# Row maxima in pairs of heads, exponentials head by head, and one accumulator for two sets of four heads

## The chip, the cores and the metric

The kernel runs on one core of one Trainium2 chip. The metric is the device time of one launch in microseconds, the median of a few runs. TensorE (PE) multiplies into PSUM, which has eight banks of 512 float32 a partition; VectorE (DVE) and ScalarE (ACT) read it; GpSimd (POOL) works on SBUF and issues the indirect transfers; SyncE (SP) issues the others.

## The reference, cut to what matters

Two layers, each with attention and a mixture of experts, over 32 sequences of 256 tokens of width 128, with 16 heads of width 8. Layer 0 adds a position bias to the scores, has an output projection and two experts a token; layer 1 has one expert a token.

```
for layer in (0, 1):
    mod = silu(c) @ wmod                       # sa, ca, ga, sb, cb, gb per sequence
    h = layernorm(x) * (1 + ca) + sa           # layer 1: a second layernorm inside attention
    q, k, v = projections of h                 # 16 heads of 8
    scores = q @ k.T * scale (+ bias)          # 256 x 256 a head
    x = x + ga * (softmax(scores) @ v ...)     # layer 0: then @ W_out
    h = layernorm(x) * (1 + cb) + sb
    x = x + gb * experts(h)                    # top 2 of 8, or top 1 of 8
```

## The kernel before, in words

Attention of a layer runs in ticks, one for each sequence, and each tick works on several sequences at once: the functions that take an offset get the sequence at(0), at(-1), at(1) and so on. Every engine has its own hand-written order of steps for a tick (the functions tick), and semaphores alone tie the engines together. All steps of an engine run in that order; a step that waits holds up all behind it.

The softmax of a head is computed in two passes. In the first (scores_a, at(0)) TensorE makes the scores with queries on the partitions, one head into one PSUM bank of two (A); VectorE takes the row maxima of each head (row_max, L869). After each eight heads VectorE splits the negated maxima into two bf16 parts (split_max), TensorE turns them (turn_max), ScalarE copies them out (max_rows), and SP sends them as two more rows of the matmul operand (stack_max, L529). In the second pass (scores_b, at(-1)) TensorE makes the transposed scores, from which the maxima are already subtracted through these rows, two heads into a two-bank buffer of two (Bp); ScalarE takes the exponentials of both at once (exps, L722) into probs. Layer 0 adds a product for the bias near the diagonal (L1147).

Then, for each four heads, weigh (L1159) multiplies by the values, whose 32 columns a head are 8 values, a one and zeros, so that four heads fill the 128 partitions of one half of M1; ScalarE copies that out (head_sums, L729); TensorE turns it (turn_heads, L1167) into the other half; and VectorE divides by the sums (normalise, L891 and L895). There is one M1, so the weigh of a set waits for the normalise of the set before.

Other steps of the tick that the text speaks of: first_stats, added_stats, inner_stats, second_stats and rms_moments (moments of rows, through aggregate); first_norm, outer_norm, inner_norm, second_norm (L824) and rms_norm; split_qk on GpSimd, which splits q and k of at(1) into bf16 parts for stack_up (L523); modulate and scatter on GpSimd; residual (L918); choose_first, choose_second, weigh_choices and place, which choose experts and count rows on VectorE. place ends its reading of M0 with the update of run (L1008), after which turn_max(at(0), 0) may write M0. TensorE's order around the start of a tick:

```
a_pass(0, 1)
chunk(0)                    # scores_b of heads 0 and 1 of at(-1); waits for stack_max's rows
a_pass(2)
heads_step(weigh, -2, 3)
...
a_pass(3)
chunk(1)
if at(1):
    ...
    project_qk(*at(1))
a_pass(4)
```

VectorE chains dependent steps with a semaphore (Chain.link, settle). In layer 1, where the next maximum's number is in MIDST, settle first issues that maximum and waits behind it, so that the gap is filled.

The expert stages use the same PSUM buffers for other products and are not changed but for the buffers' names.

## Time and profile before

| what | us |
|---|---|
| median of 3 runs | 2255.24 |
| lowest and highest of them | 2250.59, 2255.43 |
| the profiled execution's own time | 2244.62 |
| its span | 2242.8 |
| busy in the span: PE, DVE, ACT, POOL | 1757.3, 1661.7, 1038.4, 879.3 |
| attention of layer 0, about | 60 to 830 |
| attention of layer 1, about | 1155 to 1980 |

In the rows below an instruction's line is given as L and its number. Windows and timelines count from the span's start. Matmuls are pipelined: the time shown for one includes its way through the array, and consecutive ones overlap.

### The profile page before, as it was taken

What the parts mean: (1) busy time and instruction counts of PE and PEld (TensorE: products, weight loads), DVE (VectorE), ACT (ScalarE), POOL (GpSimd) and SP (SyncE); (2) the same over time, 40 slices, a digit from 0 to 9 for tenths busy, and PEclk for the clock granted to TensorE, in tenths of its full rate; (3) what the DMA queues carried; (4) which work ended last, traced back from release to release, by engine and by line L of the source; (5) the groups of instructions that cost most, each with busy time, mean ns of one, the idle gap of its engine ahead of it and who ended that gap; (6) DMA issues with size and microseconds to landing.
All of it is one profiled execution on the core that took longest, in us unless ns stands there. A gap on an engine that the chain in (4) does not pass through costs nothing. (4 is left out here: it accounts for less than half of the span.)

```text
span 2242.8 us, 55810 instructions
## 1 busy us (share of the span) xinstructions
PE 1757.3 (78%) x14626; PEld 1227.0 (55%) x14626; DVE 1661.7 (74%) x5861; ACT 1038.4 (46%) x1967; POOL 879.3 (39%) x932
## 2 busy tenths in 40 slices
PE   2588888888888847999935777878878788719997
PEld 1355555655555626999832444444444444407775
DVE  3478888888888845666626888898888888724453
ACT  0266666666666631222212555555655656603322
POOL 0224444444443333444423444444444444203333
PEclk7699999999999978999976999898998988959999
DMA  4344434343434313222245545555455454243332
GB/s 139 50 64 71 72 69 73 70 69 70 72 71 68 67 48 74 70 68 68 64 132 84 96 98 106 101 100 108 98 102 109 95 103 103 57 145 93 95 94 62
DMA packets 267157, 190.47 MB, mean 85 GB/s; under 512 B 26081, under 2 KB 257283, under 8 KB 266327
## 3 DMA queue, kind: packets, MB, share of 16 engines
q1 hardware_dynamic: 251738, 154.75, 35.4%
q0 software_dynamic: 15360, 35.03, 5.2%
q8 instruction: 26, 0.43, 0.1%
q14 instruction: 33, 0.26, 0.1%
HBM read 94.68 MB, written 53.18 MB: 66 GB/s over the span
## 5 line engine op out<-in xcount | busy, mean ns | idle before, releaser
L869 DVE TENSOR_REDUCE mx<-A 128x2 f32<-128x512 f32 x1024 | 691.6, 682 | 125.9 <-PE A L1124 94.7
L722 ACT ACTIVATE probs<-B 128x1024 f32<-128x1024 f32 x512 | 524.0, 1023 | 378.9 <-PE B L1144 205.5
L1124 PE MATMUL A<-stack 126*128 126x256 bf16 x2048 | 406.2, 286 | 162.6 <-DVE mx L869 126.5
L1144 PE MATMUL B<-stack 128*128 128x256 bf16 x2048 | 370.9, 285 | 27.2 <-DMA stack<-mrow 27.1
L1124 PEld LDWEIGHTS A<-stack 126*128 126x128 bf16 x2048 | 160.8, 99 | 340.1 <-DVE mx L869 262.5
L1159 PE MATMUL M<-probs,vals 128*32 128x256 f32 x4096 | 294.7, 405 | 23.3 <-DVE On L895 15.1
L1144 PEld LDWEIGHTS B<-stack 128*128 128x128 bf16 x2048 | 201.2, 103 | 86.1 <-issue 22.4
L631 POOL DMA_INDIRECT gathered<-h,slot_in x192 | 187.2, 975 | 154.6 <-DVE slot_in L1016 108.9
L618 POOL TENSOR_TENSOR h<-xn,back_rows 128x256 f32<-128x256 f32 x64 | 46.3, 723 | 503.5 <-DVE xn L824 503.5
L1563 PE MATMUL A<-w2s,hid 128*128 128x128 f32 x1792 | 230.4, 278 | 8.9 <-issue 8.9
L1563 PEld LDWEIGHTS A<-w2s,hid 128*128 128x128 f32 x1792 | 211.8, 192 | 18.2 <-issue 13.2
L1554 PE MATMUL B<-xtT,w1s 128*128 128x256 f32 x896 | 216.6, 395 | 5.2 <-DVE xtT L1440 2.1
L1369 POOL DMA_INDIRECT expert_out<-yt,row_dest x144 | 138.0, 959 | 177.0 <-DVE yt L1475 142.7
L1159 PEld LDWEIGHTS M<-probs,vals 128*32 128x32 f32 x4096 | 128.1, 113 | 116.3 <-issue 56.8
L1554 PEld LDWEIGHTS B<-xtT,w1s 128*128 128x128 f32 x896 | 168.2, 194 | 40.2 <-issue 16.3
L1147 PE MATMUL B<-dist,slope_ident 128*128 128x128 bf16 x1024 | 183.3, 219 | 0.0
L1523 ACT ACTIVATE hid<-B 128x1024 f32<-128x1024 f32 x72 | 73.7, 1024 | 227.9 <-PE B L1554 227.9
L594 POOL TENSOR_TENSOR parts<-qk,ones_col 128x512 bf16<-128x512 f32 x64 | 66.4, 1037 | 257.7 <-ACT qk L700 115.9
L1366 POOL DMA_INDIRECT out<-yt,row_dest x80 | 84.5, 1057 | 170.8 <-DVE yt L1480 147.2
L729 ACT ACTIVATE heads<-M 128x256 f32<-128x256 f32 x256 | 97.9, 383 | 107.2 <-PE M L1159 104.8
L1527 ACT ACTIVATE hid<-B,b 128x256 f32<-128x256 f32 x160 | 62.7, 474 | 174.3 <-PE B L1554 138.2
L668 ACT ACTIVATE rs<-mv,eps_col 128x2 f32<-128x2 f32 x192 | 56.1, 292 | 138.4 <-DVE mv L810 92.2
(190 smaller groups left out, 2847.5 us busy)
## 6 DMA issues: line engine op xcount, KB each, us to landing
stack<-parts SPq DMA_DIRECT2D x768, 64.0 KB
xt<-gathered SPq DMA_DIRECT2D x112, 132.0 KB, 2.2
probs<-gathered SPq DMA_DIRECT2D x40, 256.0 KB, 2.7
w<-in_w SPq DMA_DIRECT2D x4, 2048.0 KB
back_rows<-mod_rows SPq DMA_DIRECT2D x64, 128.0 KB, 3.3
x_mid<-X SPq DMA_DIRECT2D x64, 128.0 KB, 2.0
Y<-expert_out SPq DMA_DIRECT2D x64, 128.0 KB
X<-in_x SPq DMA_DIRECT2D x32, 128.0 KB, 2.9
```

What stands on the lines that cost most here:

```text
L631: pool.indirect_dma_start(gathered[l], bass.IndirectOffsetOnAxis(ap=slot_in[u][:, c, t:t + 1], axis=0), (h3 if l else h2)[u][:, t, :], Non ...
L722: act.activation(probs[c % 4][:, :, :, :], Bp[c % 2][:, :, :, :], ACT.Exp, scale=EXP_SCALE[l][c // 4]).then_inc(b_exp.handle, 1)
L729: act.activation(heads[g % 2][:, :], M1[:, 0:S], ACT.Copy).then_inc(o_read.handle, 1)
L869: dve.tensor_reduce(mx[u][:, h, :], A[h % 2][:, :, :], AX.X, ALU.max).then_inc(a_max.handle, 1)
L1124: ins = pe.matmul(A[h % 2][:, t, :], stack[u][0:n, h, 0, t * P:(t + 1) * P], stack[u][0:n, h, 1, :], start=True, stop=True)
L1144: ins = pe.matmul(Bp[c % 2][:, j, t, :], stack[u][:, h, 1, t * P:(t + 1) * P], stack[u][:, h, 0, :], start=True, stop=(l == 1))
L1147: ins = pe.matmul(Bp[c % 2][:, j, t, t * P:(t + 1) * P], slope_ident[:, h % HH, :], dist[:, :], start=False, stop=True)
L1159: ins = pe.matmul(M1[VW * j:VW * j + VW, 0:S], vals[u][:, t, 4 * g + j, :], probs[(2 * g + j // 2) % 4][:, j % 2, t, :], start=(t == 0), s ...
L1366: ins = pool.indirect_dma_start(expert_out[l], dest, yt[u][:, t, :], None, bounds_check=B * S - 1, oob_is_err=False)
L1369: ins = pool.indirect_dma_start(expert_out[l], dest, yt[u][:, t, :], None)
L1554: ins = pe.matmul(dst[:, f, :], w1s[u][:, f * P:(f + 1) * P], xtT[u][:, :], start=True, stop=True)
L1563: ins = pe.matmul(A[u][:, t, 0:D], hid[u][:, f, t * P:(t + 1) * P], w2s[u][:, f, :], start=(f == 0), stop=(l == 0 and f == FC - 1))
```

## The change

The buffers change places: A (scores for the maxima) becomes two buffers of two banks, Bp (scores for the exponentials) two of one bank. scores_a and row_max take two heads at once, so a tick has eight reductions of 1024 columns and not sixteen of 512. scores_b and exps take one head, so a tick has sixteen exponentials of 512 columns and not eight of 1024. Two weigh steps of four heads now add into one accumulator: the second set reads its values through a window that lies 16 columns earlier, so that its 8 values and its one land in partitions 16 to 24 of each group of 32. So head_sums, turn_heads and normalise run twice a tick for eight heads each, not four times for four, and only every second weigh waits for a normalise. The order of heads in the weights is permuted to fit. All three tick orders are rewritten, and MIDST and the counts of chained steps with them. A cut of the diff:

```diff
-DVE_MARKS = (36, 41)
-MIDST = (2, 4, 5, 7, 8, 10, 11, 13, 14)
+DVE_MARKS = (34, 39)
+MIDST = (1, 2, 4, 5, 7)
...
-        A = [ctx.enter_context(nc.psum_tensor(f"A{n}", [P, NT, S], F32)) for n in range(2)]
-        Bp = [ctx.enter_context(nc.psum_tensor(f"B{n}", [P, 2, NT, S], F32)) for n in range(2)]
+        wide = [ctx.enter_context(nc.psum_tensor(f"A{n}", [P, 2, NT, S], F32)) for n in range(2)]
+        single = [ctx.enter_context(nc.psum_tensor(f"B{n}", [P, NT, S], F32)) for n in range(2)]
...
+            def exps(b, k, u, h):
+                act.wait_ge(b_scores.handle, b_scores.after(b, h + 1))
+                c, g4 = h // 2, h // 4
+                if h % 2 == 0:
+                    act.wait_ge(pv.handle, pv.after(b, g4 - 1) if g4 >= 2 else pv.after(b - 1, g4 + 3))
+                act.activation(probs[c % 4][:, h % 2, :, :], Bp[h % 2][:, :, :], ACT.Exp,
+                               scale=EXP_SCALE[l][h // HH]).then_inc(b_exp.handle, 1)
...
-                chunk(0)
-                step(head_sums, -2, 3)
+                exp(0)
+                step(head_sums, -2, 1)
                 step(second_h, -3)
+                exp(1)
                 layer(0, first_rsqrt, 2)
-                chunk(1)
+                exp(2)
...
-                dve.tensor_reduce(mx[u][:, h, :], A[h % 2][:, :, :], AX.X, ALU.max).then_inc(a_max.handle, 1)
+                dve.tensor_reduce(mx[u][:, 2 * c:2 * c + 2, :].rearrange("p j t -> p (j t)"),
+                                  A[c % 2][:, :, :, :].rearrange("p j t s -> p (j t) s"), AX.X, ALU.max)\
+                    .then_inc(a_max.handle, 1)
...
                 step(split_max, -1, 1)
                 maxima(0, 1)
-                step(normalise, -2, 2)
+                layer(0, first_stats, 2)
                 maxima(1, 1)
-                layer(0, first_stats, 2)
-                maxima(2, 2)
                 layer(0, first_norm, 2)
                 layer(1, added_stats, 2)
-                maxima(4, 1)
-                step(normalise, -2, 3)
-                maxima(5, 1)
+                maxima(2, 1)
+                step(normalise, -2, 1)
                 step(read_logits, -3)
                 layer(1, residual, -2)
-                maxima(6, 1)
+                maxima(3, 1)
+                step(split_max, 0, 0)
                 layer(0, choose_first, -3)
                 layer(1, second_stats, -2)
                 layer(1, outer_norm, 2)
-                maxima(7, 1)
-                step(split_max, 0, 0)
-                maxima(8, 1)
-                step(normalise, -1, 0)
+                maxima(4, 1)
                 layer(1, modulate_rows, 2)
                 layer(1, gated_base, 0)
-                maxima(9, 1)
                 layer(0, choose_second, -3)
                 layer(1, choose_first, -3)
-                maxima(10, 1)
+                maxima(5, 1)
                 layer(0, residual, -2)
                 layer(1, inner_stats, 2)
-                maxima(11, 1)
                 layer(0, second_stats, -2)
                 layer(1, second_norm, -2)
-                maxima(12, 1)
-                step(normalise, -1, 1)
+                maxima(6, 1)
+                step(normalise, -1, 0)
                 step(weigh_choices, -3)
-                maxima(13, 1)
                 layer(1, rms_moments, -2)
                 step(place, -3)
-                maxima(14, 1)
+                maxima(7, 1)
                 layer(0, second_norm, -2)
                 layer(1, inner_norm, 2)
-                maxima(15, 1)
                 layer(1, rms_norm, -2)
...
                 for t in range(NT):
                     for j in range(4):
-                        ins = pe.matmul(M1[VW * j:VW * j + VW, 0:S], vals[u][:, t, 4 * g + j, :],
+                        first = (HH * q + 4 * s + j) * VW
+                        ins = pe.matmul(M1[VW * j:VW * j + VW, 0:S], vals[u][:, t, first:first + VW],
                                         probs[(2 * g + j // 2) % 4][:, j % 2, t, :],
-                                        start=(t == 0), stop=(t == NT - 1), tile_position=(0, VW * j))
+                                        start=(q == 0 and t == 0), stop=(q == 1 and t == NT - 1), tile_position=(0, VW * j))
...
-                a_pass(0, 1)
-                chunk(0)
-                a_pass(2)
+                a_pass(0)
+                b_pass(0)
+                b_pass(1)
+                a_pass(1)
                 heads_step(weigh, -2, 3)
...
-                a_pass(3)
-                chunk(1)
+                b_pass(2)
                 if at(1):
                     m0_read((h2T_read, -3))
                     project_qk(*at(1))
-                a_pass(4)
-                heads_step(turn_heads, -2, 3)
-                a_pass(5)
+                b_pass(3)
+                a_pass(2)
+                heads_step(turn_heads, -2, 1)
                 if at(-3):
                     m0_read((qk_f32, 1))
                     gate(*at(-3))
-                chunk(2)
-                a_pass(6)
+                b_pass(4)
+                b_pass(5)
+                a_pass(3)
                 if at(-1):
                     m0_read((logits_read, -3), (qk_f32, 1))
                     turn_max(*at(-1), 1)
                 heads_step(weigh, -1, 0)
-                a_pass(7)
-                chunk(3)
+                b_pass(6)
                 if at(0):
                     m0_read((mT_read, -1, 2), (qk_f32, 1))
                     project_v(*at(0))
-                a_pass(8)
-                heads_step(turn_heads, -1, 0)
+                b_pass(7)
+                a_pass(4)
```

## Rows read from the trace of the kernel before

**Rows 1.** Windows of both attention stages: window, length, busy time (count) by engine, PEclk, DMA, GB/s

```profile
205.00:700.00 495.00, 429.88 (x4354) 290.88 (x4358) 438.28 (x1442) 306.47 (x570) 214.83 (x220) 1.00 0.42 71
1280.00:1876.00 596.00, 480.74 (x4020) 284.17 (x4023) 531.76 (x1845) 348.63 (x700) 268.77 (x300) 0.90 0.51 103
```

**Rows 2.** Groups by line: layer 0's maxima, all small reductions, layer 1's exponentials and head_sums

```profile
L869 DVE TENSOR_REDUCE mx<-A 128x2 f32<-128x512 f32 x351 | 239.4, 687 | 27.0 <-PE A L1124 21.4 <-DVE xn L824 0.3
...
L956 DVE TENSOR_REDUCE r<-lg 128x2 f32<-128x16 f32 x64 | 10.4, 162 | 0.0
...
L722 ACT ACTIVATE probs<-B 128x1024 f32<-128x1024 f32 x200 | 204.8, 1024 | 168.7 <-PE B L1144 167.8
L729 ACT ACTIVATE heads<-M 128x256 f32<-128x256 f32 x100 | 38.3, 383 | 38.7 <-PE M L1159 38.4
```

**Rows 3.** Timelines of layer 1, VectorE, SP's queue and TensorE: start, duration, instruction, idle before

```profile
1518.51 0.16 DVE L1008 TENSOR_TENSOR run<-run,M 128x8 f32<-128x8 f32 x1
...
1521.23 0.69 DVE L869 TENSOR_REDUCE mx<-A 128x2 f32<-128x512 f32 x1
...
1524.39 0.69 DVE L869 TENSOR_REDUCE mx<-A 128x2 f32<-128x512 f32 x1 [0.90 <-PE A L1124]
...
1526.09 0.69 DVE L869 TENSOR_REDUCE mx<-A 128x2 f32<-128x512 f32 x1 [0.61 <-PE A L1124]
...
1529.17 0.68 DVE L869 TENSOR_REDUCE mx<-A 128x2 f32<-128x512 f32 x1
...
1542.32 0.16 DVE L1008 TENSOR_TENSOR run<-run,M 128x8 f32<-128x8 f32 x1
...
1519.81 0.69 SPq L529 DMA_DIRECT2D stack<-mrow  x1
...
1521.94 0.61 PE L1144 MATMUL B<-stack 128*128 128x256 bf16 x4 [0.52 <-DMA stack<-mrow]
...
1525.66 0.38 PE L1124 MATMUL A<-stack 126*128 126x256 bf16 x2
...
1530.95 0.38 PE L1124 MATMUL A<-stack 126*128 126x256 bf16 x2
```

**Rows 4.** Timeline of VectorE in one tick of layer 0

```profile
500.23 0.69 DVE L869 TENSOR_REDUCE mx<-A 128x2 f32<-128x512 f32 x1
...
501.81 0.47 DVE L819 BATCH_NORM_STATS2 st<-X 128x6 f32<-128x128 f32 x2
502.44 0.25 DVE L810 BATCH_NORM_AGGREGATE mv<-st 128x2 f32<-128x6 f32 x2 [0.16 <-DVEq L111]
502.75 1.29 DVE L869 TENSOR_REDUCE mx<-A 128x2 f32<-128x512 f32 x2
...
504.85 0.69 DVE L869 TENSOR_REDUCE mx<-A 128x2 f32<-128x512 f32 x1 [0.30 <-PE A L1124]
505.46 0.20 DVE L891 RECIPROCAL rsum<-M 128x8 f32<-128x8 f32 x1
...
505.83 0.68 DVE L869 TENSOR_REDUCE mx<-A 128x2 f32<-128x512 f32 x1
...
507.24 0.69 DVE L869 TENSOR_REDUCE mx<-A 128x2 f32<-128x512 f32 x1 [0.65 <-PE A L1124]
...
520.92 0.59 DVE L824 TENSOR_SCALAR xn<-X,mv,rs 128x128 f32<-128x128 f32 x2
```

**Rows 5.** Timelines of layer 0 over two ticks: VectorE, SP's queue, TensorE

```profile
204.34 0.59 DVE L824 TENSOR_SCALAR xn<-X,mv,rs 128x128 f32<-128x128 f32 x2
...
218.88 3.99 SPq L523 DMA_DIRECT2D stack<-parts  x6
...
227.53 0.39 PE L1124 MATMUL A<-stack 126*128 126x256 bf16 x2 [0.36 <-DMA stack<-parts]
```

**Rows 6.** Windows within one tick of layer 1, columns as in rows 1

```profile
1508.00:1514.00 6.00, 3.46 (x37) 1.78 (x34) 5.57 (x22) 2.58 (x5) 0.25 (x1) 0.99 0.61 98
1514.00:1520.50 6.50, 5.93 (x35) 2.80 (x36) 6.13 (x27) 2.81 (x8) 1.93 (x3) 0.50 0.67 144
```

203 lines of the change are left out of this document (103 added, 100 removed).

## The prediction, made before the change was run

> **What bounds the kernel now.** I read the windows first, the two attention stages by themselves, then the groups by line, then the timelines of one tick of either layer. In the windows the reader is to see VectorE busy for nine tenths of both stages (438 of 495 us, 532 of 596), TensorE for less, and TensorE's granted clock at 1.00 in layer 0 but 0.90 in layer 1 [rows 1]. The lines give the tick: 351 maxima at 16 a tick make layer 0's 495 us some 21.94 ticks of 22.56 us, and 200 exponentials at 8 a tick make layer 1's 596 us 25 ticks of 23.84 us [rows 1, 2]. The expert stages change only in the names of their buffers.
>
> Nine tenths busy is not yet a bound. In layer 1 the timeline closes a loop [rows 3]. VectorE's place ends its update of run at 1518.67; the row of maxima goes out on SP's queue at 1519.81; TensorE stands 0.52 us at the first exponential scores until that transfer is in, at 1521.94. Behind it, in TensorE's order, come the scores of heads 2 and 3, a weigh, a turn, more exponential scores and a projection; head 4's scores start at 1525.66, and VectorE takes their maximum at 1526.09, having waited 0.90 us for head 3 and 0.61 for head 4. From 1518.67 that is 7.42 us. Then VectorE works nearly without a pause up to the next place, which ends at 1542.48: 16.39 us. The sum, 23.81, is the tick. So layer 1 is set by 7.42 us in which TensorE and a transfer lead, and 16.39 in which VectorE does.
>
> Layer 0 has another loop, over two ticks. Its last VectorE step but one, second_norm, releases GpSimd, which modulates, scatters, waits for the scatter and only then splits the next q and k; SP issues the stack transfers, and head 0's scores of the tick after next wait for them. From second_norm's end (204.93) to those scores (227.53, idle 0.36 on that DMA) it is 22.6 us [rows 5]. About 0.55 later the first maximum starts, and from a first maximum (500.23) to second_norm's end (521.51) are 21.28 us [rows 4]. (22.6 + 0.55 + 21.28) / 2 = 22.2, against 22.56 measured: this loop nearly sets the tick.
>
> **The change part by part, for one tick.**
>
> *Maxima.* Two reductions in a row start every 0.605 us (1.29 for two, less an overlap of 0.08) [rows 4]; the 496 columns between a reduction of 512 (687 ns) and one of 16 (162 ns) cost 525 ns [rows 2], so 512 columns are some 0.54 of it. A reduction of 1024 isn't in the trace: below, 2 x 0.54 = 1.08; above, 2 x 0.605 = 1.21. I take 1.14, one fixed part of 0.07 for two. 16 x 0.605 becomes 8 x 1.14: -0.56 us of VectorE.
>
> *Normalising.* One takes 0.37 (505.46 to 505.83) [rows 4]. Two of double width replace four; 64 more columns and 8 more reciprocals add about 0.08, so 4 x 0.37 becomes 2 x 0.45: -0.58.
>
> *Exponentials.* 1024 columns take 1024 ns and the 256 of head_sums 383 [rows 2]: 0.83 ns a column and 0.17 fixed, so 512 take 0.60. Sixteen instead of eight add 1.4 us, two fewer head_sums take 0.8 away: +0.6 on an engine that is busy 62% and 58% [rows 1]. What hides it is ScalarE's own idle time, 169 us in 25 ticks before the exponentials [rows 2]; without that cover it would be +0.6. Taken as nothing. Their scores have one bank a buffer now, so TensorE waits for the exponential two heads back: 1.2 us for two, where a tick of 23 leaves 3 for each pair of heads; also nothing, and at most 0.6 where two follow each other with no other product between. TensorE loses four transposes, and no row of either loop waits for the accumulator: nothing.
>
> *Layer 1, the led part.* TensorE's order keeps the first exponential scores, and so the row transfer, ahead of pair 1's maxima scores. Up to that point nothing is shorter: 3.27 us. Behind it the same work stands in another order. Before, head 4's scores started 3.72 after it [rows 3]; now four products instead of two stand before weigh (+0.22), one exponential head falls behind the projection (+0.22), and the pair for head 4 comes with head 5 (+0.22 until it is complete). 3.27 + 3.72 + 0.43 + 0.66 = 8.08 instead of 7.42. VectorE can't use the time: place now has one maxima pair behind it (pair 0) and then needs pair 1, where heads 15, 0, 1 and 2 and a normalise were. So the stall grows as its own work shrinks.
>
> *Layer 1, VectorE's part.* Six pairs stand where eleven heads did (6.84 for 6.6: +0.24), two normalises for three (-0.1, some of them were filled). The maxima slipped into VectorE's own semaphore gaps fall from nine to five, and those left in this part leave four chains open: second_stats, choose_first, inner_stats, rms_moments. An open one takes 0.94 us of which 0.47 and 0.25 are work [rows 4], so 0.22 each: +0.9. And pair 4 (heads 8, 9) is now taken inside split_max, ahead of second_stats and outer_norm. TensorE's order lets head 8's scores start 5.29 us after head 4's (1525.66 to 1530.95) [rows 3], so pair 4 is ready 5.3 after pair 2's maxima start; VectorE is there sooner. From head 4's maximum to head 6's it took 3.08 (1526.09 to 1529.17, head 5's within); with pair 2 for the two heads (1.14 for 1.21) and a normalise wider by 0.08 that stays 3.1, and pair 3 (1.14) and the first step of split_max (0.1) make 4.4: +0.9. I take 0.3 off, since outer_norm then runs later against GpSimd's work. 16.39 + 0.24 - 0.1 + 0.9 + 0.9 - 0.3 = 18.03. The tick: 8.08 + 18.03 = 26.1, +2.3. Over some 28 full ticks of a layer (32 items less the ramps): +64 us. Bounds: below, every wait gone and only work counted: the two waits of 1.5 go and the work stays within 0.2, -1.7 a tick, -48 us; above, the clock (third rival).
>
> *Layer 0.* The work falls by 0.56 + 0.58. But second_norm now stands behind the last pair, not before head 15 (+0.6 in the loop), and first_norm meets a new wait: its reciprocal root is queued on ScalarE behind head_sums, second_h and now one more exponential of 0.6, while VectorE comes to it after two pairs instead of four heads and a normalise. I put the waits there and at pair 2 at 1.2, where 0.30 and 0.65 for scores go [rows 4]. 21.28 + 0.6 - 1.14 - 0.95 + 1.2 = 21.0; the loop halves the difference: -0.15. From the VectorE side alone, 1.14 would be saved. Between the two I take -0.3, nearer the loop, since that wait is in the trace: -8 us. Bounds: -1.14 x 28 = -32, and +10 if the new waits are twice as long.
>
> *TensorE's clock.* In layer 1 the granted clock is 0.99 from 1508 to 1514, where TensorE is busy 3.46 of 6 us, and then 0.50, the level of 1.2 GHz, to 1520.5 [rows 6]. That low stretch ends before the led part's products (1521.94), so it costs nothing now. The Trainium skill, page "TensorE: Matmul & The Clock Gate", section "Part 1: The HAM clock gate", says that activity releases the throttle and idle time brings it back; the traced drop agrees. By that rule a longer stall makes more low stretches, in the led part too, and the sum would be that of the third rival instead of the one here.
>
> **Sum.** +64 - 8 = +56. The profiled execution took 2244.6 us, of which 2242.8 is its span; so 2301. The three runs lie 6 to 11 above it; with 8 added, 2309.
>
> **The rivals.** *The saved work arrives.* For it: VectorE is the busiest engine of both stages [rows 1], and maxima buffers of four heads let TensorE run further ahead. Then layer 0 gains 1.1 and layer 1 its 0.2 and half of the waits, 0.9: -31 - 25 = -56, so 2245 - 56 + 8 = 2197. It decides if pair 2's scores are in when VectorE is through pairs 0 and 1: 2.56 us after place less head 15's 0.6 (1521.23 against 1518.67 [rows 3]), two pairs and 0.4 of statistics, 4.6 in all, and not 8. Against it: the transfer alone takes 3.27 of that.
>
> *It cancels.* Layer 0 gains the full 1.1 (-31), layer 1 loses only half (+29), because ScalarE's shorter first exponential and outer_norm out of GpSimd's way shorten it: 2251.
>
> *The clock falls into the led part.* The stretch from the first exponential scores to pair 2, of whose 4.8 us some 4.4 are products, takes that much longer at 1.2 GHz: +4.4 a tick, +123 us beyond the forecast if every tick of layer 1 is hit, half that if every other one is: 2371 to 2432. For it: the stalls of layer 1 grow; against it: the dense work just before the transfer.
>
> **How the numbers follow.** Forecast 0.54, the saved work 0.20, cancelling 0.12, the clock 0.14. The likeliest time is 2309, by itself 2275 to 2350. The range of 2205 to 2390 leaves out half of the first rival's 0.20 (that the saved work arrives in full) and half of the clock's 0.14. Under 0.2%, some 4.5 us, this kernel's runs can't tell a change from none. Faster: 0.20 and part of cancelling, 0.26. Same: 0.06. Slower: 0.68.
>
> **What would show it.** Right: in layer 1 the first exponential scores still wait for the row transfer, VectorE waits over 1 us before pair 1 and about 2 before pair 2, and the tick is near 26 us; in layer 0 first_norm waits for the reciprocal root, and the tick is 22 to 22.5. Maxima of 1024 columns last near 1.22 us (1.14 from start to start), exponentials near 0.60. Wrong: a layer 1 tick under 23.8, pair 2 ready before VectorE asks, or a granted clock under 0.8 over layer 1's ticks.

## The result, and the profile after

The changed kernel takes 2448.4 us (median of 4 runs, 2443.8 to 2451.4) where the kernel before takes 2252.9 in the same session: a ratio of 1.0866 with a 95% interval of 1.0842 to 1.0889. The sign was forecast (slower, 0.68). The size was not: 2309 us with a range up to 2390, so some 140 us of the loss were missed, more than half of it in layer 0.

The page's busy time, then the groups by line over the whole span: how many, busy us and mean ns, idle time of the engine before them and what ended it. The last two lines are the kernel before.

```profile
PE 1794.6 (73%) x14370; PEld 1234.7 (51%) x14370; DVE 1632.8 (67%) x5093; ACT 1027.0 (42%) x2351; POOL 880.4 (36%) x932
```

```profile
L882 DVE TENSOR_REDUCE mx<-A 128x4 f32<-128x1024 f32 x512 | 623.4, 1218 | 286.5 <-PE A L1127 253.6 <-issue 26.6
L729 ACT ACTIVATE probs<-B 128x512 f32<-128x512 f32 x1024 | 590.0, 595 | 288.8 <-PE B L1148 160.8 <-PE B L1145 123.3
L1145 PE MATMUL B<-stack 128*128 128x256 bf16 x2048 | 449.5, 300 | 150.8 <-ACT probs L729 109.0 <-DMA stack<-mrow 38.9
L907 DVE TENSOR_TENSOR On<-M,rsum 128x128 f32<-128x128 f32 x128 | 36.8, 287 | 3.3
L906 DVE RECIPROCAL rsum<-M 128x16 f32<-128x16 f32 x128 | 32.1, 250 | 22.9 <-PE M L1171 14.4 <-issue 5.9 <-DVE mv L823 2.6
```

```profile
L869 DVE TENSOR_REDUCE mx<-A 128x2 f32<-128x512 f32 x1024 | 691.6, 682 | 125.9 <-PE A L1124 94.7 <-issue 23.6 <-DVE xn L824 0.3
L1144 PE MATMUL B<-stack 128*128 128x256 bf16 x2048 | 370.9, 285 | 27.2 <-DMA stack<-mrow 27.1
```

VectorE has less work than before (1632.8 us against 1661.7), and the new instructions last what was forecast: 1218 ns for maxima of 1024 columns, 595 for an exponential of 512, about half a microsecond for a division (0.45 forecast). What grew is waiting: 286.5 us before maxima, where it was 125.9, and 109.0 us in which TensorE's exponential scores wait for ScalarE's exponentials, where the kernel before has no such wait.

The windows of full ticks, 24 of layer 0 and 22 of layer 1, cut at VectorE's update of run (columns as in [rows 1]); first the changed kernel, then the kernel before:

```profile
234.73:841.55 606.82, 486.71 (x4676) 324.19 (x4668) 483.13 (x1290) 333.18 (x766) 234.96 (x240) 0.93 0.37 63
1475.91:2089.73 613.82, 443.17 (x3462) 252.49 (x3454) 450.68 (x1364) 300.53 (x749) 237.02 (x264) 0.79 0.45 87
```

```profile
225.39:768.57 543.18, 471.58 (x4778) 319.12 (x4778) 480.62 (x1578) 335.52 (x622) 234.36 (x240) 1.00 0.42 70
1375.40:1900.31 524.91, 428.44 (x3542) 252.52 (x3542) 468.82 (x1628) 306.95 (x617) 236.52 (x264) 0.89 0.50 102
```

So layer 0's tick is 606.82 / 24 = 25.28 us and layer 1's 613.82 / 22 = 27.90. The kernel before has 22.63 (granted clock 1.00) and 23.86 (0.89). Over 28 ticks a layer that is +74 us and +113 us, 187 of the 199 by which the spans differ. The prediction had -8 and +64.

One tick of layer 1, the rows that answer to [rows 3], in timelines of VectorE, ScalarE, SP's queue and TensorE:

```profile
1560.59 0.16 DVE L1020 TENSOR_TENSOR run<-run,M 128x8 f32<-128x8 f32 x1
...
1566.87 1.23 DVE L882 TENSOR_REDUCE mx<-A 128x4 f32<-128x1024 f32 x1 [0.82 <-PE A L1127]
...
1570.61 1.23 DVE L882 TENSOR_REDUCE mx<-A 128x4 f32<-128x1024 f32 x1 [2.12 <-PE A L1127]
...
1588.37 0.16 DVE L1020 TENSOR_TENSOR run<-run,M 128x8 f32<-128x8 f32 x1
```

```profile
1561.84 0.60 ACT L729 ACTIVATE probs<-B 128x512 f32<-128x512 f32 x1 [0.81 <-PE B L1145]
1562.34 0.36 ACT L721 ACTIVATE mrow<-M 16x256 bf16<-16x256 bf16 x1
```

```profile
1562.72 0.69 SPq L535 DMA_DIRECT2D stack<-mrow  x1
```

```profile
1559.16 1.93 PE L1163 MATMUL M<-probs,vals 128*32 128x256 f32 x16 [2.29 <-DVE On L907]
1560.89 0.38 PE L1134 MATMUL M<-ident_b,mneg 128*16 128x128 bf16 x2
1561.20 0.61 PE L1145 MATMUL B<-stack 128*128 128x256 bf16 x2
...
1565.05 1.03 PE L1145 MATMUL B<-stack 128*128 128x256 bf16 x4 [0.27 <-DMA stack<-mrow]
```

The reader is to see four distances. From the end of the update (1560.75) to the rows' transfer on SP: 1.97 us, where it was 1.14. From there to the first exponential scores: 2.33 (2.13). From those to pair 2's maxima: 5.56 (4.15 before, 4.81 forecast). From pair 2 to the end of the next update, VectorE's part: 17.92 (16.39 before, 18.03 forecast). VectorE's part came out as predicted; the led part is 9.86 us, not 8.08. Over the 22 ticks the mean led part is 10.14 us (7.36 before), the mean of VectorE's part 17.76 (16.50). ScalarE's two rows show why the first distance grew: the copy of the rows (L721) stands behind head 14's exponential, whose scores TensorE makes only after the turn that the copy reads. The windows of the same tick show the rest:

```profile
1546.00:1556.40 10.40, 6.89 (x70) 4.12 (x59) 9.01 (x29) 5.50 (x14) 2.57 (x3) 1.00 0.51 81
1556.40:1566.30 9.90, 6.33 (x37) 2.93 (x35) 7.05 (x25) 3.66 (x10) 5.17 (x7) 0.50 0.52 131
```

The granted clock is at its lower level, 1.2 GHz, from before the third weigh (1.93 us where others take 1.07) to the scores of pair 1. In the tick of before the low stretch ended ahead of the first exponential scores [rows 6]. From the transfer to pair 2 the granted clock is 0.73 in the mean of the 22 ticks, where it was 0.94.

Layer 0, the groups by line over its 24 ticks, VectorE's and then TensorE's; the last line is TensorE's in the kernel before:

```profile
L882 DVE TENSOR_REDUCE mx<-A 128x4 f32<-128x1024 f32 x192 | 235.0, 1224 | 52.8 <-PE A L1127 47.7
L837 DVE TENSOR_SCALAR xn<-X,mv,rs 128x128 f32<-128x128 f32 x94 | 28.3, 343 | 37.5 <-ACT rs L675 37.5
L969 DVE TENSOR_TENSOR rt<-lg,r 128x16 f32<-128x16 f32 x24 | 25.5, 1062 | 0.8
L983 DVE TENSOR_SCALAR h<-token_ids 128x2 f32 (+1 forms) x24 | 19.1, 797 | 0.0
L972 DVE TENSOR_TENSOR rt<-rev_iota,h 128x16 f32<-128x16 f32 x24 | 12.7, 530 | 0.8
```

```profile
L1127 PE MATMUL A<-stack 126*128 126x256 bf16 x768 | 124.4, 287 | 0.0
L1145 PE MATMUL B<-stack 128*128 128x256 bf16 x768 | 175.1, 288 | 55.0 <-ACT probs L729 41.2 <-DMA stack<-mrow 13.9
L1097 PE MATMUL M<-ident,xn 128*128 128x128 f32 x48 | 11.7, 330 | 24.3 <-ACT mrow L721 24.3
```

```profile
L1124 PE MATMUL A<-stack 126*128 126x256 bf16 x769 | 147.1, 275 | 47.5 <-DVE mx L869 40.8 <-DMA stack<-parts 4.8
```

By the windows, VectorE's busy time in the 24 ticks is 483.13 us where it was 480.62, and its idle time 123.7 where it was 62.6. So waiting makes 61.1 of the 63.6 us, 2.55 of the tick's 2.65. Two waits make 59.3 of it: the maxima wait 52.8 us for scores (30.6 before, same cut), and first_norm waits 37.5 us for its reciprocal root (0.4), 1.55 more a tick.

The work that maxima and divisions save does not show in the busy time, because others took it up. Three small steps of choose_first, 0.17 us each where nothing disturbs them, take 25.5 + 19.1 + 12.7 = 57.3 us (26.3 before) beside GpSimd's split of q and k, while two other steps, which lay beside it before, got shorter (15.2 + 12.2 us to 8.4 + 4.0).

TensorE's lines say which path the tick is on. Before, TensorE waited 4.8 us for the stack transfers, with which the prediction's two-tick loop ends, and never for the rows of maxima. Now it waits 0.0 us for the stack transfers, but 13.9 us for the row transfer, 24.3 for the copy of the rows (the turn of the next xn goes into M0 too) and 41.2 for exponentials. So TensorE no longer waits for that loop at all.

### The profile page after: what moved, and what is told of

The parts are those of the page before. It is cut to its first block and busy times, and to the rows that moved or that the text cites. A ratio compares the mean times of both kernels' runs of the same rounds, so it can differ in the third digit from the quotient of the medians.

```text
span 2442.0 us, 53983 instructions
## 1 busy us (share of the span) xinstructions
PE 1794.6 (73%) x14370; PEld 1234.7 (51%) x14370; DVE 1632.8 (67%) x5093; ACT 1027.0 (42%) x2351; POOL 880.4 (36%) x932
## 5 line engine op out<-in xcount | busy, mean ns | idle before, releaser
L882 DVE TENSOR_REDUCE mx<-A 128x4 f32<-128x1024 f32 x512 | 623.4, 1218 | 286.5 <-PE A L1127 253.6
L729 ACT ACTIVATE probs<-B 128x512 f32<-128x512 f32 x1024 | 590.0, 595 | 288.8 <-PE B L1148 160.8
L1145 PE MATMUL B<-stack 128*128 128x256 bf16 x2048 | 449.5, 300 | 150.8 <-ACT probs L729 109.0
L1127 PE MATMUL A<-stack 126*128 126x256 bf16 x2048 | 354.3, 302 | 33.5 <-DMA stack<-parts 27.3
L1565 PE MATMUL B<-w2s,hid 128*128 128x128 f32 x1792 | 230.4, 278 | 8.6 <-issue 8.6
L1565 PEld LDWEIGHTS B<-w2s,hid 128*128 128x128 f32 x1792 | 211.8, 192 | 17.9 <-issue 12.9
L1556 PE MATMUL A<-xtT,w1s 128*128 128x256 f32 x896 | 216.4, 395 | 5.3 <-DVE xtT L1442 2.0
L1556 PEld LDWEIGHTS A<-xtT,w1s 128*128 128x128 f32 x896 | 168.2, 194 | 40.1 <-issue 16.3
L1525 ACT ACTIVATE hid<-A 128x1024 f32<-128x1024 f32 x72 | 73.7, 1024 | 227.8 <-PE A L1556 227.8
L1529 ACT ACTIVATE hid<-A,b 128x256 f32<-128x256 f32 x160 | 62.7, 474 | 174.2 <-PE A L1556 135.8
```

The lines of the kernel that those rows point to most:

```text
L729: act.activation(probs[c % 4][:, h % 2, :, :], Bp[h % 2][:, :, :], ACT.Exp, scale=EXP_SCALE[l][h // HH]).then_inc(b_exp.handle, 1)
L882: dve.tensor_reduce(mx[u][:, 2 * c:2 * c + 2, :].rearrange("p j t -> p (j t)"), A[c % 2][:, :, :, :].rearrange("p j t s -> p (j t) s"), AX ...
L1127: ins = pe.matmul(A[c % 2][:, j, t, :], stack[u][0:MROW, 2 * c + j, 0, t * P:(t + 1) * P], stack[u][0:MROW, 2 * c + j, 1, :], start=True, ...
L1145: ins = pe.matmul(Bp[h % 2][:, t, :], stack[u][:, h, 1, t * P:(t + 1) * P], stack[u][:, h, 0, :], start=True, stop=(l == 1))
L1525: act.activation(hid[u][:, :, :], src, ACT.Relu).then_inc(hidden.handle, 1)
L1556: ins = pe.matmul(dst[:, f, :], w1s[u][:, f * P:(f + 1) * P], xtT[u][:, :], start=True, stop=True)
```

## The experiments

Theories: R, the rows' copy behind an exponential makes the led part late; Q, ScalarE's order holds TensorE up through one-bank buffers; O and O2, TensorE's order of pairs 1 and 2; K, the lower clock by itself; G, GpSimd beside choose_first; S, sharing the accumulator saves; W, the third weigh at the low clock holds the turn of the rows. The table gives each kernel's ratio to the kernel before on the same chip, and its mean ticks, cut as above from one trace.

| kernel | ratio, 95% interval | layer 0 tick, clock | layer 1 tick, clock |
|---|---|---|---|
| before | 1 | 22.63, 1.00 | 23.86, 0.89 |
| changed | 1.0866 (1.0842 to 1.0889) | 25.28, 0.93 | 27.90, 0.79 |
| rows_first | 1.0513 (1.0481 to 1.0545) | 24.68, 0.93 | 25.84, 0.83 |
| pair1_first | 1.0849 (1.0831 to 1.0867) | 25.57, 0.92 | 27.29, 0.81 |
| busy_pe | 1.1088 (1.1052 to 1.1123) | 25.80, 0.91 | 28.94, 0.88 |
| shared_only | 0.9964 (0.9947 to 0.9980) | 22.41, 1.00 | 23.91, 0.95 |
| rows_root | 1.0413 (1.0377 to 1.0448) | 23.89, 0.95 | 25.87, 0.84 |
| rows_pair2 | 1.0546 (1.0518 to 1.0574) | 25.44, 0.91 | 25.60, 0.83 |
| rows_choose | 1.0442 (1.0416 to 1.0469) | 24.16, 0.95 | 25.73, 0.83 |
| rows_all | 1.0369 (1.0344 to 1.0395) | 23.87, 0.96 | 25.57, 0.83 |
| sums_early | 1.0525 (1.0505 to 1.0546) | 23.31, 0.98 | 27.29, 0.75 |
| before_late | 1.0777 (1.0753 to 1.0802) | 25.44, 0.97 | 27.28, 0.87 |
| act_before | 1.0447 (1.0430 to 1.0465) | 23.90, 1.00 | 26.14, 0.83 |
| act_dve_before | 1.0324 (1.0300 to 1.0348) | 22.79, 1.00 | 26.00, 0.83 |
| order_before | 1.0192 (1.0174 to 1.0211) | 22.85, 0.99 | 25.27, 0.81 |
| order_late | 1.0610 (1.0577 to 1.0642) | 23.46, 0.97 | 27.28, 0.75 |
| order_plain | 1.0329 (1.0307 to 1.0352) | 22.85, 0.99 | 26.14, 0.83 |

The ticks of one trace differ: the changed kernel's in layer 0 run from 23.7 to 27.1 us. busy_pe leaves layer 0's program as it is, and its mean there is 0.52 longer. So half a microsecond between two means of such a layer says little by itself.

### rows_first: the copy ahead of head 14's exponential

```diff
+                step(max_rows, 0, 0)
                 exp(14)
-                step(max_rows, 0, 0)
                 exp(15)
```

> The changed kernel with one step moved on ScalarE: the copy of the first half's rows of maxima goes ahead of the exponential of head 14, not behind it. Theory R (late rows): head 14's scores stand behind the turn of those rows on TensorE, so the copy waits for scores and an exponential that it doesn't need (0.9 us in a layer 0 tick, about 1 in a layer 1 tick, where those scores run at the lower clock level), and the row transfer, pair 1 and all that follows are late by as much. Then both layers' ticks fall by some 0.8 us: about 45 us in all, 2400 us. Theory K (clock): layer 1's loss is mostly TensorE's lower clock in the led part, and layer 0's the waits before it; then the copy's 0.9 us is taken up by the wait for the division, and the gain is under 15 us.

From 8.7% to 5.1% above before: some 79 us of 2243, more than the 45 expected. Timelines of VectorE, SP's queue and TensorE in layer 1:

```profile
1492.68 0.16 DVE L1020 TENSOR_TENSOR run<-run,M 128x8 f32<-128x8 f32 x1
...
1500.81 1.22 DVE L882 TENSOR_REDUCE mx<-A 128x4 f32<-128x1024 f32 x1 [1.42 <-PE A L1127]
...
1493.87 0.69 SPq L535 DMA_DIRECT2D stack<-mrow  x1
...
1495.99 0.61 PE L1145 MATMUL B<-stack 128*128 128x256 bf16 x4 [0.78 <-DMA stack<-mrow]
```

The distances are 1.03, 2.12 and 4.82: the led part is 7.97 us, where the prediction worked out 8.08 from 3.27 and 4.81. The first exponential scores take 0.61 us again, not 1.03: with the earlier copy they no longer lie at the low clock level. Over the 22 ticks the led part is 8.09 us in the mean, not 10.14, and VectorE's part 17.76 in both: the whole gain of 2.06 lies in the led part. Of it, 0.97 comes up to the transfer (0.99 for 1.96); the rest comes behind it, where the granted clock is 0.87 and not 0.73. So R holds for layer 1, and the extra gain over R's price is clock. In layer 0 the tick fell by 0.6 only, which is near what two traces differ by.

### before_late: the same step in the kernel before

```diff
-                step(max_rows, 0, 0)
                 chunk(7)
+                step(max_rows, 0, 0)
```

> The kernel before with one step moved on ScalarE, as the change has it: the copy of the first half's rows behind the last exponential, not ahead of it. Theory R (late rows): that exponential's scores stand behind the turn of the rows on TensorE, so the copy is late by those scores and the exponential: some 1.3 us from turn to copy in layer 1 and 1.6 in layer 0, less the 0.3 that the copy waits now. Layer 1's loop runs through the copy, so its tick grows by about 1.2 us (34 us in all); layer 0's two-tick loop takes half: 0.6 (17 us): about 2300 us, 2 to 2.5% over the kernel before. Rival: the copy only matters together with the one-bank buffers; then the time stays within 0.5% of before.

7.8% slower, three times what R's price gave, and nearly the loss of the whole change. Layer 1, VectorE, ScalarE, SP's queue, TensorE:

```profile
1555.86 0.16 DVE L1008 TENSOR_TENSOR run<-run,M 128x8 f32<-128x8 f32 x1
...
1565.58 0.69 DVE L869 TENSOR_REDUCE mx<-A 128x2 f32<-128x512 f32 x1 [0.64 <-PE A L1124]
...
1557.01 1.02 ACT L722 ACTIVATE probs<-B 128x1024 f32<-128x1024 f32 x1 [0.39 <-PE B L1144]
1557.93 0.36 ACT L715 ACTIVATE mrow<-M 16x256 bf16<-16x256 bf16 x1
...
1558.31 0.69 SPq L529 DMA_DIRECT2D stack<-mrow  x1
...
1560.44 1.03 PE L1144 MATMUL B<-stack 128*128 128x256 bf16 x4 [0.23 <-DMA stack<-mrow]
```

The transfer comes 2.29 us after the update instead of 1.14, as R says; from the first exponential scores (2.13 later) to head 4's maximum it is then 5.14 us, not 4.15 [rows 3], at a granted clock of 0.57 from 1559 to 1563. So a microsecond of lateness bought another microsecond of slow products: the first exponential scores take 1.03 us, not 0.61. This tick is one of the short ones (26.2; they go up to 29.1). Over the 22 ticks the led part is 10.79 us in the mean, not 7.36, and VectorE's part 16.50 in both, so the whole 3.4 us lie in the led part: 1.6 up to the transfer (2.62 for 1.04) and 1.9 behind it, at a granted clock of 0.74 for 0.94. In layer 0 the tick grew by 2.8, not 0.6: the maxima wait 83.9 us in 24 ticks where they waited 30.6, and choose_first's three steps take 57.0 us, not 26.3. The two-tick loop that was to halve such a delay did not; here too TensorE waits 0.0 us for its transfers, but 34.5 for the copy of the rows.

### pair1_first: pair 1's scores ahead of the transfer

```diff
                 a_pass(0)
+                a_pass(1)
                 b_pass(0)
                 b_pass(1)
-                a_pass(1)
```

> The changed kernel with TensorE's scores of pair 1 ahead of the first two heads' exponential scores, so that they don't wait for the row transfer. Theory O (order, the prediction's): pair 1's 0.6 us (1.06 at the lower clock) leaves the stretch between the transfer and pair 2, the wait before pair 1's maxima (0.45 us in layer 0, 0.9 in layer 1) goes, and both ticks fall by 0.6 to 0.9 us: 35 to 45 us in all, about 2405 us. Rival: pair 1 is not on the path that sets the tick, since pair 2 waits for weigh and the turn behind it and first_norm for its reciprocal root; then under 10 us.

1.0849 against 1.0866, intervals overlapping: no gain. Layer 1's tick is 0.6 us shorter, the low end of what O gave it; layer 0's is 0.3 longer, which two traces of the same program can differ by. Theory O falls as the cause of the loss.

### busy_pe: repeated products to hold the clock

```diff
                 heads_step(turn_heads, -1, 0)
+                again(12, 6)
...
+                again(14, 8)
                 heads_step(weigh, -1, 2)
```

> The changed kernel with work added, in layer 1 alone: TensorE repeats the scores of head 12 six times ahead of count and those of head 14 eight times ahead of the third weigh (each again into the buffer that the real scores overwrite), where it otherwise waits 1.7 and 2.3 us. The output is the same. Theory K (clock): the granted clock, 0.50 for some 10 us of every layer 1 tick from the third weigh to pair 1, then stays at or near 1.00 there; A's and B's scores, the weigh and the turns of the led part take half as long, and the tick falls from 27.8 by 1.3 to 2 us, 36 to 56 us in all: about 2400 us. Rival: what releases the led part is the row transfer and place, not TensorE's speed; then the clock rises and the time stays within 10 us, or grows where the repeats last longer than the waits.

again(h, n) makes the exponential scores of head h n times over, in layer 1 alone. It came out slower, 10.9% above before, although the granted clock of layer 1 rose from 0.79 to 0.88. The repeats filled the waits (0.34 us were left before count, 0.73 before the third weigh, which ran in 1.07), but the low stretch only came later. The window and TensorE's timeline behind it:

```profile
1548.00:1555.00 7.00, 6.03 (x35) 3.20 (x36) 3.26 (x7) 2.09 (x6) 4.20 (x5) 0.52 0.50 99
```

```profile
1550.93 1.03 PE L1145 MATMUL B<-stack 128*128 128x256 bf16 x4 [0.57 <-DMA stack<-mrow]
1551.76 1.06 PE L1127 MATMUL A<-stack 126*128 126x256 bf16 x4
1552.75 1.94 PE L1163 MATMUL M<-probs,vals 128*32 128x256 f32 x16
```

It now covers the led part from 1548 to 1555, its weigh too (1.94, where it took 1.07 at 1566.76 in the changed kernel), and pair 2 comes 10.84 us after the update (1557.48 - 1546.64), not 9.86. Over the 22 ticks the led part grows by 1.04 (11.18), as much as the tick. The lower clock does lengthen products, as K says, but what counts is which products lie in the low stretch, not how long it is on average. No run of the changed kernel held the clock up through the led part, so what K is worth by itself isn't shown.

### rows_root, rows_choose, rows_pair2, rows_all: moves on top of rows_first

```diff
 rows_root (ScalarE)
-                layer(0, second_rsqrt, -2)
                 exp(11)
                 exp(12)
+                layer(0, second_rsqrt, -2)
 rows_choose (VectorE)
-                layer(0, choose_first, -3)
...
                 maxima(4, 1)
+                layer(0, choose_first, -3)
 rows_pair2 (TensorE)
                 heads_step(weigh, -2, 3)
+                a_pass(2)
...
                 b_pass(3)
-                a_pass(2)
 rows_all: these three, and on ScalarE
                 exp(0)
+                layer(0, first_rsqrt, 2)
                 step(head_sums, -2, 1)
                 step(second_h, -3)
                 exp(1)
-                layer(0, first_rsqrt, 2)
```

> The changed kernel with the rows' copy ahead of head 14's exponential (as in the run before, 2356 us, 5.1% above the kernel before) and one more step moved on ScalarE, in layer 0: second_norm's reciprocal root goes behind the exponentials of heads 11 and 12, not ahead of them. Theory Q (queue on ScalarE): the root waits 2.2 us for its moments, head 11's exponential waits behind it, and with one bank a buffer head 13's scores (and pair 7, the third weigh and the turn behind them) wait 1.35 us for that exponential; TensorE's idle time there brings its clock to 0.50 in most ticks. Without it the low stretches of layer 0 get fewer and its tick falls from 24.7 by 0.5 to 1 us: 14 to 28 us. Rival: the turn of the rows waits for place on VectorE anyway, which ends at about the same time; then under 5 us.

> The changed kernel with the rows' copy moved as before (2356 us), and in layer 0 choose_first behind pair 4 on VectorE, not ahead of it. Theory G (GpSimd): choose_first takes 3.6 us beside GpSimd's split of q and k, where three of its instructions of 0.17 us last 0.7 to 1.1; a reduction from PSUM lasts 1.22 there as everywhere. With the reduction under the split and choose_first mostly behind it, the tick falls by 0.8 to 1.5 us: 22 to 42 us. Rival: choose_second and count come as late as before, since the whole order is VectorE's; or the split then lengthens another step by as much: under 8 us.

> The changed kernel with the rows' copy moved as before (2356 us), and TensorE's scores of pair 2 right behind the weigh of the older sequence, ahead of the turn, the exponential scores and the projection of q and k. Theory O2 (order of pair 2): the led part ends when pair 2's scores are in, and these six products stand ahead of them for no reason of the buffers; in layer 1 VectorE's wait of 1.4 us before pair 2 goes (pair 2 is then ready before VectorE has done the added moments), in layer 0, where first_norm waits for its reciprocal root until 0.36 us before pair 2, only that 0.36: (1.4 + 0.36) x 28 = about 49 us less, 2307 us. Rival: what is pushed back (projection of q and k, on which GpSimd's split and the next stack hang) becomes the new bound; under 15 us.

> The three moves of this call together on the changed kernel with the rows' copy moved, and in layer 0 first_norm's reciprocal root ahead of head_sums and second_h on ScalarE (its wait of 1.4 us before first_norm then goes, since its moments are in before the exponential of head 0 ends). If R, Q, O2 and G hold and add up: layer 0 falls from 24.7 to about 22 us a tick (root 0.7, first_norm 1.3 with pair 2's move, choose_first 1), layer 1 from 25.5 to about 24: 2356 - 75 - 42 = about 2240, no slower than the kernel before. Rival: each gain meets the same next wait (place and the turn of the rows); then the sum is no more than the best of the three by itself, near 2310.

rows_root did what was expected: layer 0's tick fell from 24.68 to 23.89, layer 1's stayed. rows_choose gave less: 24.16, 0.5 us a tick and some 16 us in all, where 22 to 42 were expected. In rows_root TensorE's wait for exponentials in layer 0 falls from 39.9 us (24 ticks) to 8.9; Q holds. rows_pair2 failed: layer 1 gained 0.24, not 1.4. Pair 2 did come earlier (the led part is 6.48 us in the mean, not 8.09), but VectorE's part grew from 17.76 to 19.12: the division behind pair 2 now waits 14.7 us in the 22 ticks, not 1.8, and the logits 6.8, not 0.0. Layer 0 lost 0.76, as the projection behind it came later: gate then waits 13.6 us for ScalarE's q and k, and first_norm 42.8 instead of 33.0. rows_all gave 3.7%, not parity: first_norm no longer waits in layer 0 (33.0 to 0.0 us), but the maxima wait 52.1 us where they waited 34.9. The gains do not add; most of one wait came back as the next.

### sums_early: the first division ahead of pair 6

```diff
+                step(normalise, -1, 0)
                 maxima(6, 1)
-                step(normalise, -1, 0)
```

> The changed kernel with the rows' copy and layer 0's second reciprocal root moved (2343 us, 4.1% above before), and the division of the first accumulator ahead of pair 6 on VectorE, not behind it (in layer 1 pair 7 had been slipped in before its second half). Theory W (third weigh): in layer 1 TensorE waits 1.9 to 2.3 us for that division before the third weigh, its clock is 0.50 there, and weigh takes 1.93 us, which holds the turn of the rows; with the division 2.4 us earlier the clock stays up and the turn waits for place alone: layer 1's tick falls by 0.3 to 0.8 us, 8 to 22 us. Rival: place on VectorE releases the turn at the same time, and the low stretch only moves elsewhere; within 5 us.

Worse by 1.1 points on rows_root: layer 0 gains (23.89 to 23.31), layer 1 loses 1.4 us. Layer 1, a window and TensorE's timeline:

```profile
1512.00:1524.00 12.00, 9.84 (x61) 4.62 (x65) 9.38 (x33) 5.28 (x13) 5.65 (x7) 0.50 0.50 124
```

```profile
1514.37 1.94 PE L1163 MATMUL M<-probs,vals 128*32 128x256 f32 x16
1518.08 0.37 PE L1134 MATMUL M<-ident_b,mneg 128*16 128x128 bf16 x2 [1.77 <-DVE run L1020]
...
1522.90 1.78 PE L1163 MATMUL M<-probs,vals 128*32 128x256 f32 x16
```

The third weigh came early and ran at the low level all the same; TensorE then stood 1.77 us before the turn, nearer to the led part, and the first exponential scores and the weigh behind them ran at 0.50. The whole 1.4 us lie in the led part (9.53 in the mean for 8.12). Theory W falls, as K's forecast did in busy_pe.

### shared_only: one part of the change on the kernel before

The vals layout, weigh, head_sums, turn_heads and normalise of the change; buffers, maxima, exponentials and orders of before. The edit is shown against the kernel before.

```diff
-                step(normalise, -2, 2)
...
-                step(normalise, -2, 3)
+                step(normalise, -2, 1)
...
-                step(normalise, -1, 0)
...
-                step(normalise, -1, 1)
+                step(normalise, -1, 0)
```

> The kernel before with one part of the change alone: two sets of four heads share an accumulator, so head_sums, turn_heads and normalise run twice a tick and not four times; buffers, maxima, exponentials and the rest of the orders are those of before. Theory S (sharing saves): VectorE loses some 0.58 us of work a tick and ScalarE 0.8; layer 0 keeps its two-tick loop and gains 0.3 at most, layer 1 gains 0.2 to 0.5: 2225 to 2250 us, no slower than before. Rival: the third weigh, which then waits for a later division, brings the loss (the wait of 2.3 us before it in the changed kernel); then it is slower than before by over 20 us.

0.9964: about 8 us faster than before, of which layer 0's tick (22.41) gives 0.22 x 28 = 6. S holds in layer 0, and this version beats both kernels, by a little that the interval sets apart from nothing. In layer 1 the 0.2 to 0.5 did not come: VectorE's part is 0.37 us shorter in the mean (16.13), the led part 0.42 longer (7.78). Half a microsecond less work on VectorE a tick is worth 0.2 in layer 0 and nothing in layer 1.

### act_before, act_dve_before, order_before: the orders put back

ScalarE's, then also VectorE's, then also TensorE's order of before, with the changed buffers, reductions, exponentials and accumulators. With VectorE's order goes the list of maxima slipped into its waits, MIDST. The core of the edits:

```diff
 act_before (ScalarE; each old chunk(c) becomes exp(2c), exp(2c+1) at its place)
                 exp(0)
+                exp(1)
                 step(head_sums, -2, 1)
...
+                exp(11)
                 layer(0, second_rsqrt, -2)
-                exp(11)
                 exp(12)
...
+                step(max_rows, 0, 0)
                 exp(14)
-                step(max_rows, 0, 0)
 act_dve_before (VectorE)
-MIDST = (1, 2, 4, 5, 7)
+MIDST = (2, 3, 4, 5, 6, 7)
...
                 layer(0, choose_first, -3)
                 layer(1, second_stats, -2)
                 layer(1, outer_norm, 2)
+                maxima(3, 1)
+                step(split_max, 0, 0)
                 layer(1, modulate_rows, 2)
                 layer(1, gated_base, 0)
+                maxima(4, 1)
 order_before (TensorE; scores of both heads of a pair of exponentials side by side)
                 b_pass(2)
+                b_pass(3)
                 if at(1):
                     m0_read((h2T_read, -3))
                     project_qk(*at(1))
-                b_pass(3)
```

> The changed kernel with ScalarE's whole order put back to that of before (each exponential of two heads as two of one head at the same place): the rows' copy ahead of heads 14 and 15, layer 0's second reciprocal root ahead of heads 12 and 13, the rest as it was. VectorE's and TensorE's orders stay the changed ones. If all of the loss beyond the prediction sits in ScalarE's order, layer 1's tick is 25.5 us as with the copy alone moved, layer 0's 23.5 to 24: 2320 to 2345 us, 3 to 4.3% over the kernel before. If the order is no more than the rows' copy, it is the 2356 us (5.1%) of that run again; if the sixteen exponentials themselves cost, the same.

> The changed kernel with ScalarE's and VectorE's orders put back to those of before, TensorE's as changed. ScalarE's alone gave 4.5% above the kernel before, all three 1.9%. If VectorE's order (when each pair, the split and the division come) brings the difference, this is at 2 to 2.7%; if TensorE's (the three exponential scores that it moved behind other products: heads 3, 7, 9 and 15), it stays at 4 to 4.7%.

> The changed buffers, reductions, exponentials and accumulators, but all three orders (VectorE, ScalarE, TensorE) of before, step for step: a pair of maxima stands where the odd head of the pair stood on VectorE and where the even one stood on TensorE, two exponentials where one of two heads stood, and the slipped maxima are pairs 2 to 7. If the orders bring the loss, this is no slower than before, 2200 to 2250 us, since it has 0.5 us a tick less VectorE work. If the buffers do (a pair is ready only when both heads are, one-bank exponentials tie TensorE to ScalarE), it stays over 2% above the kernel before, 2290 to 2350 us.

Put back in this order, ScalarE's is worth 4.2 points, VectorE's 1.2, TensorE's 1.3, and 1.9 stay: most of the loss is the orders', but not all, and act_dve_before at 3.2% lies between its two cases. In layer 0 VectorE's order does it (23.90 to 22.79): first_norm waits 0.1 us in 24 ticks, not 6.8, and choose_first's three steps take 22.5 us, not 58.3, because pair 3 and the split come behind it. TensorE's order gives layer 1 its 0.7. The groups by line of order_before:

```profile
L882 DVE TENSOR_REDUCE mx<-A 128x4 f32<-128x1024 f32 x512 | 623.3, 1219 | 163.4 <-PE A L1127 134.5 <-issue 24.5
...
L1145 PE MATMUL B<-stack 128*128 128x256 bf16 x2048 | 387.9, 295 | 32.5 <-DMA stack<-mrow 32.1
```

TensorE's products no longer wait for an exponential here, with the same one-bank buffers: the 109.0 us of the changed kernel were the orders' doing.

### order_late and order_plain: two single steps on order_before

```diff
 order_late (ScalarE)
-                step(max_rows, 0, 0)
                 exp(14)
+                step(max_rows, 0, 0)
 order_plain
-MIDST = (2, 3, 4, 5, 6, 7)
+MIDST = ()
```

> The kernel with the new buffers and all orders of before (1.9% above the kernel before), and the one step changed on ScalarE: the rows' copy behind the exponential of head 14. Theory R: this step by itself brings most of the loss; with one-bank buffers it is late by one exponential of 0.6 and its two to four products instead of 1.0 and twice as many, so about half of what it cost the kernel before (7.8%): 3 to 5% more, 5 to 7% above before in all. Rival: the step costs only where the other orders leave the led part on the path; then under 1% more.

> The kernel with the new buffers and all orders of before (1.9% above the kernel before), and in layer 1 no maxima slipped into VectorE's own semaphore waits (six pairs were). The prediction's price for an open chain is 0.22 us: 6 x 0.22 = 1.3 us a layer 1 tick, 37 us in all, about 2325 us. Rival: the waits of layer 1 for pairs absorb it, since the same pairs then come later and their scores are in; under 10 us.

order_late is 6.1% above before: the one step takes 4.2 points here, 7.8 in the kernel before, 3.5 in the changed one. order_plain costs 0.87 us a layer 1 tick (25.27 to 26.14), 0.15 for each open chain where 0.22 was expected, and nothing in layer 0, where nothing is slipped in.

## Why the prediction was wrong in size, point by point

Two steps failed: in layer 1 the term of 3.27 us at the head of the led part, and in layer 0 the loop that was taken to go on setting the tick.

- **Maxima, divisions, exponentials by themselves.** Right: 1218 ns, 250 + 287 ns, 595 ns. They were the part that the trace priced well, and the smallest.
- **"Taken as nothing" for the exponentials.** Wrong. ScalarE has time enough, and order_before shows that one-bank buffers need no wait. But scores now wait for the exponential two heads back, and in the changed order the second reciprocal root and other steps stand between two exponentials and wait for VectorE; such a wait now reaches TensorE. The term was priced by ScalarE's load where its order decides: 0.79 us of layer 0's tick (rows_root, on top of rows_first), and the next point.
- **Layer 1, the led part: "Up to that point nothing is shorter: 3.27 us."** This step failed. Nothing was shorter, but it was longer: 4.30 (1.97 + 2.33). The diff puts max_rows behind exp(14); the prediction counted ScalarE's steps and did not follow this one along the path it had drawn itself. With it undone 3.15 and 4.82 are measured for the 3.27 and 4.81 forecast, and 8.09 in the mean for 8.08. So the sign was not luck in layer 1: with the copy back in its place the stall that the prediction described is there.
- **Layer 1, VectorE's part.** Right in the sum, 17.92 for 18.03, and partly by luck in the terms. Open chains leave three gaps of 0.16 a tick, 0.47 for the 0.9 (order_plain puts one at 0.15 for 0.22). Two steps that were not priced nearly cancel: by the means of the 22 ticks residual takes 0.6 less and split_max's first step 0.7 more; outer_norm takes 0.5 less, where 0.3 was taken off. Eleven heads at 0.605 are 6.66, not 6.6, which changes little.
- **Layer 1's tick.** 27.90 for 26.1; 25.84 in rows_first.
- **The clock, the third rival (0.14).** It came in, though not as the rival priced it (+4.4 a tick): by the rows of that tick, 0.75 + 0.20 us of the led part beyond the copy's lateness. The trace shows the granted clock at 0.50 there, and rows_first shows it gone from the first exponential scores. In that stretch products took 1.03 us for 0.61 and 0.95 for 0.60, and the clock rose again before the weigh, so much less than 4.4 was lost. "A granted clock under 0.8" was named as a sign that the forecast fails; it was 0.79.
- **Layer 0: "nearer the loop", -0.3.** This step failed too. Wrong by 2.95 us a tick, the largest miss. The two-tick loop was no cover: in the changed kernel TensorE waits 0.0 us for its transfers, and before_late lengthened layer 0 by 2.8. What the tick does follow is the row copy (2.8 by before_late, 0.6 by rows_first), ScalarE's second root (0.8) and VectorE's order (1.1). That these add up to the 2.65 is not shown: rows_all shows that such gains do not add. first_norm's wait was foreseen but priced at a part of the 1.2 for all waits; it alone is 1.55. choose_first beside GpSimd's split was not foreseen; it takes up the work that was to be saved.
- **choose_first beside GpSimd.** The Trainium skill, page "SBUF — State Buffer", section "SBUF: two separate sides", says that VectorE and GpSimd share one port pair, held for a whole instruction, and that a VectorE operation needs it in a two-port mode or with two SBUF inputs. The trace agrees for the comparison with two SBUF inputs (L969, 1062 ns beside the split, 175 elsewhere), and maxima from PSUM keep their 1.22 us beside it. The write of token ids (L983) has one SBUF input and is held as well, 797 ns in the mean; whether it runs in a two-port mode no run here shows. In one tick of layer 0 of the changed kernel (VectorE, then GpSimd) each of the two ends as GpSimd's instruction does:

```profile
551.30 1.10 DVE L983 TENSOR_SCALAR h<-token_ids 128x2 f32 x1
...
552.51 1.02 DVE L969 TENSOR_TENSOR rt<-lg,r 128x16 f32<-128x16 f32 x1
...
551.19 1.18 POOL L601 TENSOR_TENSOR rem<-qk,parts 128x512 f32<-128x512 f32 x1
552.45 1.04 POOL L602 TENSOR_TENSOR parts<-rem,ones_col 128x512 bf16<-128x512 f32 x1
```

  Moving the steps out does not gain all that they lose: from act_before to act_dve_before the three steps fall by 1.5 us a tick (58.3 to 22.5 us in 24), but split_max and choose_second come beside the split instead (their first steps take 36.2 for 18.2 and 15.2 for 4.0 us), VectorE's busy time falls by 0.76 a tick, and the tick by 1.11.
- **What stays open.** order_before is 1.9% above before and sharing alone 0.4% below, so larger maxima and single exponentials cost about 2.3 points under the old orders if the parts add; in layer 1 that cost lies in the led part, 8.68 us in the mean for 7.36, with VectorE's part at 16.58 for 16.50. Which of the two buffers brings it isn't shown, and a better order for them was not found.

## What to carry to other kernels

Follow each small copy that feeds a transfer through the new order of its engine, not only through its load: one copy of 0.36 us, moved behind one exponential, cost 7.8%, though that engine idles two fifths of the attention stages [rows 1]. When an order is rewritten together with the buffers, put the old orders back one engine at a time; that separated 6.7 of 8.7 points from the buffers, in the order in which the three were put back. Don't price a wait by what it holds up alone: in this kernel a later transfer also moved the low clock stretch onto the products behind it.

## What the runs showed of the hardware

Adding products to keep TensorE busy raised the mean granted clock of layer 1 from 0.79 to 0.88 and lengthened its tick by 1.04 us; moving a wait of TensorE (sums_early) lowered it from 0.84 to 0.75. In both the stretch at 1.2 GHz moved further onto the led part. The mean granted clock alone says little of the time: shared_only's trace has layer 1 at 0.95 instead of 0.89 with the same tick (23.91 against 23.86), and executions of the kernel before lie between 0.911 and 0.942 over the whole span with times from 2236.9 to 2256.1 us that do not follow it (0.911 at 2242.2, 0.935 at 2239.1).
